# The first cross attention of a decoder kernel: a group of 13 steps ordered as seven blocks

## The reference, cut to what matters

```python
q = (x @ w_q).reshape(B, SQ, N_HEADS, D_HEAD)
k = (cond @ w_k).reshape(B, SKV, N_HEADS, D_HEAD)
v = (cond @ w_v).reshape(B, SKV, N_HEADS, D_HEAD)
attn = jnp.einsum('bqhd,bkhd->bhqk', q, k) * scale
attn = jax.nn.softmax(attn, axis=-1)
out = jnp.einsum('bhqk,bkhd->bqhd', attn, v).reshape(B, SQ, N_HEADS * D_HEAD)
return out @ w_out + b_out
```

## Time and profile before

| what | value |
|---|---|
| three runs, median (lowest to highest) | 3449.01 us (3447.76 to 3451.31) |
| profiled execution, span of its instructions | 3459.0 us (no time of its own is given beside the span) |
| TensorE matmuls busy | 3138.3 us, 91% |
| VectorE busy | 2354.6 us, 68% |
| ScalarE busy | 1708.5 us, 49% |
| GpSimd busy | 1731.8 us, 50% |
| mean granted TensorE clock | 0.956 |

### The profile page before, as it was taken

How to read it: one execution, slowest core, us unless ns; L and a number is a source line. 1 busy time by engine, 2 the same in 40 slices (tenths; PEclk the granted TensorE clock), 3 DMA queues, 4 the chain that set the end, 5 groups by cost and what they waited for, 6 DMA issues and landing times. The chain is left out here.

```text
span 3459.0 us, 62575 instructions
## 1 busy us (share of the span) xinstructions
PE 3138.3 (91%) x24201; PEld 1810.0 (52%) x24201; DVE 2354.6 (68%) x4987; ACT 1708.5 (49%) x2102; POOL 1731.8 (50%) x1163
## 2 busy tenths in 40 slices
PE   7999999989999999999999953958989999999797
PEld 3666666644555555555555523846654434444346
DVE  5999999945655665566656556156429978888518
ACT  3888888823434444444444441222234656666641
POOL 5999999814777777777777831322460000000012
PEclk9999999989999999999999976988997999999898
DMA  2000000020000000000000054730021111120101
GB/s 70 6 2 2 2 2 2 26 55 1 4 1 4 1 4 4 1 4 1 4 1 1 1 160 136 239 86 1 1 43 18 18 18 18 18 26 10 33 1 37
DMA packets 65530, 91.51 MB, mean 26 GB/s; under 512 B 9586, under 2 KB 55539, under 8 KB 64371
## 3 DMA queue, kind: packets, MB, share of 16 engines
q1 hardware_dynamic: 61682, 83.17, 9.5%
q0 software_dynamic: 3072, 4.34, 0.7%
q10 hardware_dynamic: 512, 0.26, 0.0%
HBM read 62.34 MB, written 10.65 MB: 21 GB/s over the span
## 5 line engine op out<-in xcount | busy, mean ns | idle before, releaser
L969 DVE TENSOR_REDUCE x0hm<-x0pM 128x1 f32<-128x400 f32 (+1 forms) x1024 | 520.8, 563 | 378.3 <-PE x0pM L871 378.2
L434 POOL TENSOR_SCALAR rows<-rows,mb 128x1024 bf16<-128x1024 bf16 x512 | 567.5, 1119 | 98.1 <-DVE mb L382 98.1
L376 DVE TENSOR_SCALAR_CACHE_REDUCE rows<-pS 128x1024 bf16<-128x1024 f32 x512 | 605.8, 1209 | 2.0 <-PE pS L312 1.5
L445 ACT ACTIVATE prT<-pP 128x1024 bf16<-128x1024 bf16 x512 | 521.9, 1024 | 110.1 <-PE pP L323 92.6
L1433 DVE TENSOR_REDUCE x1hm<-x1pM 128x1 f32<-128x400 f32 (+1 forms) x1024 | 519.1, 567 | 67.4 <-PE x1pM L1319 64.2
L1552 ACT ACTIVATE x1pr<-x1pST 128x1024 f32<-128x1024 f32 (+1 forms) x416 | 403.8, 1022 | 216.1 <-PE x1pST L1371 216.0
L831 POOL TENSOR_TENSOR x0acc<-x0acc,x0pr 128x1024 f32<-128x1024 f32 (+1 forms) x176 | 422.1, 2398 | 110.2 <-ACT x0pr L1080 95.0
L831 POOL TENSOR_TENSOR x0acc<-x0acc,o_nat 128x1024 f32<-128x1024 f32 (+1 forms) x176 | 419.1, 2381 | 72.3 <-ACT o_nat L1080 53.5
L1080 ACT ACTIVATE x0pr<-x0pST 128x1024 f32<-128x1024 f32 (+1 forms) x208 | 212.9, 1024 | 279.6 <-PE x0pST L915 279.6
L1080 ACT ACTIVATE o_nat<-x0pST 128x1024 f32<-128x1024 f32 (+1 forms) x208 | 213.0, 1024 | 278.4 <-PE x0pST L915 278.0
L2666 POOL MEMSET f_tri<- 128x128 f32 x1 | 0.2, 209 | 675.7 <-POOLq L1224 675.7
(11 more groups left out here) (367 smaller groups left out, 5125.2 us busy)
## 6 DMA issues: line engine op xcount, KB each, us to landing
m_w<-in_moe_w1T SPq DMA_DIRECT2D x16, 1024.0 KB
m_w<-in_moe_w2T SPq DMA_DIRECT2D x16, 1024.0 KB, 9.1
acc_d<-m_zero SPq DMA_DIRECT2D x8, 514.0 KB, 9.5
m_acc<-acc_d SPq DMA_DIRECT2D x8, 514.0 KB, 5.6
x1sq<-x1qh SPq DMA_DIRECT2D x32, 128.0 KB, 4.0
x1sk<-x1kh SPq DMA_DIRECT2D x32, 100.1 KB, 3.6
rows_d<-m_xr SPq DMA_DIRECT2D x1, 2176.0 KB, 9.0
g_xN<-in_x SPq DMA_DIRECT2D x1, 2048.0 KB
```

The costliest lines, as they stand in the source:

```text
L376: nc.vector.tensor_scalar(rows[u][:, half * 1024:(half + 1) * 1024], pS[half][:, :], 1.0, None, ALU.mult, ALU.max, accum_out=mx[u][:, half ...
L434: nc.gpsimd.tensor_scalar(r, r, -1.0, mb[u][:, 0:1], ALU.mult, ALU.add).then_inc(s_df, 1)
L445: nc.scalar.activation(prT[u][:, half * 8:(half + 1) * 8, :], pP[half][:, :, :], ACT.Exp, scale=-1.0 / HD ** 0.5).then_inc(s_ex, 1)
L969: emptied(nc.vector.tensor_reduce(hm[g % 2][:, a, t, i % 8 // 2:i % 8 // 2 + 1], bank(name)[:, 0:w], AX.X, ALU.max, negate=True), name)
```

## The change

A group's 13 steps become seven blocks. Block 0 has step 0 and the value products of the last two steps of the group before; block b has the score steps 2b - 1 and 2b back to back and the value products of the two steps before these (in block 1 of step 0 alone). In each block come the scores, then two or three maxima (`FRONT`), then at most one unit of another kind (`whole`), then the value products, then two more maxima (`BACK`, none in block 6). The query unit is in block 1, the sum in 2, keys in 3 and 4, and both output units of the group before in 5 and 6. The shift follows its maximum as before; this is the first maximum of block 4. The lists of VectorE and ScalarE follow; reciprocals are in blocks 3 and 4, one ahead of and one behind the last two maxima, and the normalising product is at the end of block 4. Which matmuls, reductions and copies there are, and their shapes, is unchanged.

```diff
--- before.py
+++ after.py
@@ -666,46 +666,48 @@
     MX = 4 * len(PIECES) * 2
     AHEAD = 16
     NP = 4
-
-    def done(g, kt):
-
-        if g < 0:
-            return MX + AHEAD
-        return min(GROUPS * MX, MX * (g + 1) + AHEAD + ((kt + 1) * MX) // NK)
-
-    def units_in(g, kt):
-
+    BLOCKS = [([0], [-2, -1])] + [([2 * b - 1, 2 * b], [2 * b - 3, 2 * b - 2] if b > 1 else [0]) for b in range(1, 7)]
+    FRONT, BACK = [2, 3, 3, 3, 3, 3, 3], [2, 2, 2, 2, 2, 2, 0]
+
+    def whole(g, b):
+
+        if b == 1 and g + 2 < GROUPS:
+            return [("q", g + 2)]
+        if b == 2 and g >= 1:
+            return [("sum", g - 1)]
+        if b in (3, 4) and g // 4 + 1 < H // 2 and g % 4 < 2:
+            return [("k", g // 4 + 1, 2 * (g % 4) + b - 3)]
+        if b in (5, 6) and g >= 1:
+            return [("out", g - 1, b - 5)]
+        return []
+
+    def maxima(g, b, back):
+
+        before = MX * (g + 1) + AHEAD + sum(FRONT[:b]) + sum(BACK[:b]) + (FRONT[b] if back else 0)
         units = []
-        before = done(g, kt - 1) if kt else done(g - 1, NK - 1)
-        for i in range(before, done(g, kt)):
+        for i in range(before, min(before + (BACK if back else FRONT)[b], GROUPS * MX)):
             units.append(("max", i))
             if i % MX == 3 and i > MX:
                 units.append(("shift", i // MX - 1))
-        if done(g, kt) == GROUPS * MX > before:
+        if g == GROUPS - 2 and b == 5 and back:
             units.append(("shift", GROUPS - 1))
-        if kt == 1 and g + 2 < GROUPS:
-            units.append(("q", g + 2))
-        if kt == 3 and g >= 1:
-            units.append(("sum", g - 1))
-        if kt == 11 and g >= 1:
-            units.append(("out", g - 1, 0))
-        if kt == 0 and g >= 2:
-            units.append(("out", g - 2, 1))
-        if g // 4 + 1 < H // 2 and g % 4 < 2 and kt in (5, 9):
-            units.append(("k", g // 4 + 1, 2 * (g % 4) + kt // 9))
         return units
+
+    def units_in(g, b):
+
+        return maxima(g, b, False) + whole(g, b) + maxima(g, b, True)
 
     first = [("k", 0, r) for r in range(4)] + [("q", 0), ("q", 1)]
     later = [("v", t, a) for t in range(6, NC_) for a in range(2)]
-    for i in range(done(-1, 0)):
+    for i in range(MX + AHEAD):
         first.append(("max", i))
         if i % 3 == 0 and i // 3 < len(later):
             first.append(later[i // 3])
         if i == MX + 3:
             first.append(("shift", 0))
     number, count = {}, 0
-    last = [("out", GROUPS - 2, 1), ("sum", GROUPS - 1), ("out", GROUPS - 1, 0), ("out", GROUPS - 1, 1)]
-    for name in first + [n for g in range(GROUPS) for kt in range(NK) for n in units_in(g, kt)] + last:
+    last = [("sum", GROUPS - 1), ("out", GROUPS - 1, 0), ("out", GROUPS - 1, 1)]
+    for name in first + [n for g in range(GROUPS) for b in range(7) for n in units_in(g, b)] + last:
         number[name] = count
         count += 1
 
@@ -934,16 +936,17 @@
                 pe_.wait_ge(s_set, 5)
                 for name in first:
                     unit(name)
-                for n in range(STEPS):
-                    kt = n % NK
-                    scores(n)
-                    for name in units_in(n // NK, kt):
-                        unit(name)
-                    if kt == 1:
-                        values(n - 1)
-                    elif n and kt % 2 == 1 or n and kt == 0:
-                        values(n - 2)
-                        values(n - 1)
+                for g in range(GROUPS):
+                    for b, (steps, products) in enumerate(BLOCKS):
+                        for kt in steps:
+                            scores(g * NK + kt)
+                        for name in maxima(g, b, False) + whole(g, b):
+                            unit(name)
+                        for kt in products:
+                            if g or kt >= 0:
+                                values(g * NK + kt)
+                        for name in maxima(g, b, True):
+                            unit(name)
                 values(STEPS - 2)
                 values(STEPS - 1)
                 for name in last:
@@ -1026,21 +1029,25 @@
 
                 for name in first:
                     unit(name)
-                for n in range(STEPS):
-                    g, kt = n // NK, n % NK
-                    for name in units_in(g, kt):
-                        unit(name)
-                    if g and 5 <= kt < 9:
-                        reciprocals(g - 1, kt - 5)
-                    elif g and kt == 9:
-                        normalise(g - 1)
-                    if g >= GROUPS - 2 and kt < 4:
-                        statistics(4 * (g - GROUPS + 2) + kt)
-                unit(last[0])
+                for g in range(GROUPS):
+                    for b in range(7):
+                        for name in maxima(g, b, False) + whole(g, b):
+                            unit(name)
+                        if g and b in (3, 4):
+                            reciprocals(g - 1, 2 * b - 6)
+                        for name in maxima(g, b, True):
+                            unit(name)
+                        if g and b in (3, 4):
+                            reciprocals(g - 1, 2 * b - 5)
+                        if g and b == 4:
+                            normalise(g - 1)
+                        if g >= GROUPS - 2 and b < 2:
+                            statistics(4 * (g - GROUPS + 2) + 2 * b)
+                            statistics(4 * (g - GROUPS + 2) + 2 * b + 1)
                 for i in range(4):
                     reciprocals(GROUPS - 1, i)
                 normalise(GROUPS - 1)
-                for name in last[2:]:
+                for name in last[1:]:
                     unit(name)
 
             @block.scalar
@@ -1089,15 +1096,17 @@
                         wait_filled(act, name)
                         emptied(nc.scalar.activation(v_all[0:r, t, a * 512:(a + 1) * 512], bank(name)[0:r, :], ACT.Copy),
                                 name)
-                for n in range(STEPS):
-                    exponentials(n)
-                    for name in units_in(n // NK, n % NK):
-                        if name[0] in ("q", "k"):
-                            high(name)
-                        elif name[0] == "sum":
-                            sums(name)
-                    if n and n % NK == 0:
-                        copy_out(n // NK - 1)
+                for g in range(GROUPS):
+                    for b, (steps, _) in enumerate(BLOCKS):
+                        for kt in steps:
+                            exponentials(g * NK + kt)
+                        for name in whole(g, b):
+                            if name[0] in ("q", "k"):
+                                high(name)
+                            elif name[0] == "sum":
+                                sums(name)
+                        if g and b == 0:
+                            copy_out(g - 1)
                 copy_out(GROUPS - 1)
                 sums(("sum", GROUPS - 1))
```

## The result

The changed kernel takes 3490.73 us (median of four runs, 3488.81 to 3492.69); the kernel before, run beside it, 3450.16. The ratio is 1.0108 (95% interval 1.0092 to 1.0125): 40.6 us slower, against a forecast of 35 us slower and 3484. The profiled execution of the changed kernel took 3490.84 us.

A forecast was written before the change was run, and what follows sets the result against it. TensorE's instruction stream bounds the stage; only waits change. Key groups 13 x 1.53 plus plain 16 x 1.09 give 37.3, less 2 is +35 on 3459.0: 3494, or 3484 us with the 10 us profile difference; range 3458 to 3504.

The forecast's parts named there:

- The wait on the bank: On TensorE, a unit needing the bank of the third before it starts 1.01 us after the block's first maximum.
- The blocks: Lengths of a plain group's seven new blocks on TensorE, summing to 37.79 us against 36.70, 1.09 us more a group.
- unseen step from value product to maximum: Start of blocks after the first: switch absent from the trace, charged the scores' restart, 0.09 in a 2.14 us lead.
- Block 5: Output unit starts 1.68 us after its first maximum, held by VectorE's reciprocal and product; block 6.75 us.
- Key groups: 13 of groups 1 to 29, those with key units: each 1.53 us longer, against 1.09 for plain groups.
- the -2 charged: First group and last two together: -2 us, bounds -4 and +1, as GpSimd's final chain of additions begins earlier.
- The clock: TensorE's granted clock in the stage: stays at 1.00 despite the new short waits, so nothing charged.
- the rival: Clock falls at TensorE's waits, as the skill's rule says: 3583 us at one tenth of the stage; chance 0.03.
- the 10 us between the profiled span before and its median: Profiled span 3459.0 against median 3449.01; difference assumed to carry over, taking the forecast from 3494 to 3484 us.
- the product was not hidden: Rival: VectorE's normalising product costs nothing in block 5, unit at 1.01; 20 us less, 3464; chance 0.12.
- The faster one: Rival: units find their banks free because splitting five maxima spreads VectorE's work; 74 us less, 3375; chance 0.06.
- the point named for it: Faster rival's test: whether the first reduction is over 0.46 us after its matmul starts.

## Why the prediction was right, point by point

- **The wait on the bank** (1.01): measured 1.00 to 1.03 in blocks 1, 2 and 6. That it causes the loss is shown by the two runs that place the unit behind the values: plain groups fall to 35.21.
- **The blocks**: predicted 3.16, 6.07, 5.87, 4.47, 5.39, 6.75, 6.08; by the starts above 3.17, 6.07, 5.89, 4.46, 5.39, 6.67, 6.09. The unseen step from value product to maximum, taken with a restart, made the lead 2.14; it is 2.15.
- **Block 5** was 0.08 too long (1.68; 1.60 here, 1.56 in the median plain group), and it came that near by luck, from two errors of opposite sign. The product takes 0.70 to the next start, and I had 0.90 from a row whose 0.97 held a part of a GpSimd addition. And the product, which needs the reciprocal's result, starts 0.98 after the reciprocal (1107.13 to 1108.11); I had 0.86 from a row behind which a reduction follows, which needs no such result.
- **Key groups**: 1.53 predicted, 1.38 and 1.39 measured (40.65 to 42.03, 39.32 to 40.71). Of the difference 0.08 is block 5's. Groups 1 to 29 together grew by 35.6 instead of 37.3; what surrounds them gave back 2.0. That this is the -2 charged is luck: the end of the stage, from group 30 on, gave back 3.7, and its start took 1.6 more, with the clock at 0.50 for a while; in the second profile of the changed kernel, without that fall, it is 3.8 in all.
- **The clock** stayed at 1.00 with these stops, but for the 6.8 us at the start of the loop, which the second profile does not have. The prediction leaned on the stretch from 756 to 808 us as nothing but maxima held by their banks; that was a misreading, since projections of keys, queries and values lie there too, and TensorE's idle rows there wait for ScalarE's copies of the values. That the stage itself had run at 1.00 was the argument that held. The rule that the prediction cited from the Trainium skill on the clock gate did not bite here; the clock did fall in two experiments with longer or denser stops, so the rival was open and only unlikely.
- **What was off**: I let the 10 us between the profiled span before and its median carry over. The changed kernel's profiled execution lay at its median (3490.84 and 3490.73), so the 3494 before that step was the nearer number. The later medians of the kernel before (3456.07 to 3458.78) lie near that profile's span too: the 10 us were mostly scatter of the first runs.
- **The rivals**: the product was not hidden, since the unit started 1.60 after its maximum and not 1.01. The faster one failed at the point named for it: a bank is free 1.0 us after its matmul starts, where work alone needs 0.46. Its price was real: 3375 was worked out for banks found free, and 3401 was reached by letting the value products cover the wait.

## What to carry to other kernels

With few banks in rotation, count for each unit the distance to the instruction whose bank it reuses, and compare it with the reader's whole turnaround, not with its throughput: in these runs splitting the burst of maxima paid only where long work lay inside that distance. Moving a unit behind such work also moves the reader's part of it, so look at what stands behind that part in the reader's list, and put there first what is already ready.

## What the hardware showed unexpectedly

- A VectorE product of two SBUF operands took 2.58 us (median) beside GpSimd's additions and 0.69 without them.
- The clock stayed at 1.00 through stops of 0.5 to 1.3 us in four blocks of seven, and was granted at 0.50, the lower level, behind three stops of 0.38, 0.20 and 0.84 close together. Behind one stop of 1.2 us it fell in 12 plain groups of 16 and stayed up in four; a fall made the group 1.6 us longer.
- One matmul in one half of the array costs nothing beyond the restart when scores follow (lead 1.95 where a pair makes it 2.15).
